# Fourteen expert tiles moved from the expert stage into the last fourteen attention groups

## The reference

```python
B, T, D, H = 8, 512, 256, 16            # batch, tokens, width, heads (16 wide each)
x  = hidden_states                                              # float16
a  = layernorm(x)
q, k, v = heads((a @ wq.T + bq) / 4), heads(a @ wk.T + bk), heads(a @ wv.T + bv)
s  = q @ k.T + causal mask (-10000 above the diagonal)
o  = softmax(s, float32).astype(float16) @ v
x  = x + layernorm(o @ wo.T + bo)
t  = layernorm(x)                                               # (4096, 256)
w, idx = top_k(t @ Ws + bs, 2); w = softmax(w)                  # 8 experts, 2 per token
y  = sum over the two experts e of  w_e * ((silu(t @ Wg[e]) * (t @ Wu[e])) @ Wd[e])   # F = 688
out = x + layernorm(y)
```

## Time and profile before

| what | value |
|---|---|
| median of 3 runs | 1003.47 us (1001.8 to 1004.06) |
| profiled execution, its own time | 1003.02 us |
| its span | 1001.3 us |
| attention groups 18 to 31 | 334.0 to 527.5 us |
| routing of the last batch, table, first rows | 527.5 to 575.6 us |
| 39 expert tiles | 575.6 to 947 us |
| combine | from 947 us |

### The profile page before, as it was taken

One profiled execution on the slowest core, in us unless ns is written; L12 is line 12 of the kernel. 1 busy time (PEld: TensorE's weight loads), 2 busy tenths in 40 slices (PEclk: granted clock), 3 DMA queues, 4 the chain that ended last, 5 costly groups with the idle time before them and its releaser, 6 DMA issues. The chain is left out here.

```text
span 1001.3 us, 22338 instructions
## 1 busy us (share of the span) xinstructions
PE 824.3 (82%) x6606; PEld 472.7 (47%) x6607; DVE 670.9 (67%) x2625; ACT 549.9 (55%) x1007; POOL 414.9 (41%) x428
## 2 busy tenths in 40 slices
PE   3488787799999999999982099999999999999800
PEld 1122232233333333333331087877877877877600
DVE  5667788888888988888864345555555555555535
ACT  4588877665565565556561044555555455455325
POOL 3565645562534534253445322333323323333316
PEclk9555555555555555555555599999999999999955
DMA  5344232228000101000011242323323323233164
GB/s 160 117 126 129 88 112 65 70 79 301 29 27 23 33 17 38 2 17 27 15 30 33 79 112 39 47 36 43 43 36 47 42 37 47 37 42 47 22 199 147
DMA packets 69219, 66.17 MB, mean 66 GB/s; under 512 B 5536, under 2 KB 62752, under 8 KB 69152
## 3 DMA queue, kind: packets, MB, share of 16 engines
q1 hardware_dynamic: 55872, 50.86, 16.7%
q0 software_dynamic: 13280, 14.49, 10.6%
HBM read 34.04 MB, written 31.29 MB: 65 GB/s over the span
## 5 line engine op out<-in xcount | busy, mean ns | idle before, releaser
L580 ACT ACTIVATE pT<-bank 128x512 f16<-128x512 f32 (+1 forms) x384 | 200.4, 530 | 161.9 <-PE bank L949 160.0
L691 DVE CUSTOM_DVE_ANT_0 unused<-bank,mask 128x384 f16<-128x384 f32 (+3 forms) x512 | 234.6, 483 | 73.9 <-PE bank L940 71.4
L1231 POOL DMA_INDIRECT expert_rows<-y_sb,dest x78 | 121.5, 1558 | 263.4 <-DVE y_sb L1350 224.1
L949 PE MATMUL bank<-qT,kT 32*128 32x384 f16 (+3 forms) x512 | 203.0, 449 | 23.8 <-ACT pT L580 23.6
L940 PE MATMUL bank<-kT,qT 32*128 32x384 f16 (+3 forms) x512 | 201.0, 446 | 16.8 <-DVE nmax L691 15.9
L1390 PE MATMUL bank<-xT,gu_part 128*128 128x256 f16 (+1 forms) x1716 | 202.7, 276 | 4.8 <-issue 3.8
L1390 PEld LDWEIGHTS bank<-xT,gu_part 128*128 (+1 forms) x1716 | 168.7, 100 | 36.8 <-issue 7.7
L1415 PE MATMUL bank<-wd_part,h 128*128 (+2 forms) x1326 | 163.6, 273 | 1.2 <-ACT h L1268 0.2
L482 POOL TENSOR_SCALAR_AFFINE_SELECT pT<-pT 128x512 f16<-128x512 f16 x128 | 79.8, 635 | 155.6 <-ACT pT L580 155.1
L1415 PEld LDWEIGHTS bank<-wd_part,h 128*128 128x128 f16 (+2 forms) x1326 | 117.2, 97 | 37.5 <-issue 24.5
L1268 ACT ACTIVATE h<-hid 128x512 f16<-128x512 f32 (+2 forms) x156 | 81.7, 523 | 89.0 <-DVE hid L1330 86.6
(11 more groups left out here) (150 smaller groups left out, 925.9 us busy)
## 6 DMA issues: line engine op xcount, KB each, us to landing
expert_rows<-clear SPq DMA_DIRECT2D x1, 8192.0 KB, 26.8
stage<-wg SPq DMA_DIRECT2D x8, 688.0 KB, 4.0
stage<-wu SPq DMA_DIRECT2D x8, 688.0 KB, 4.1
stage<-wd SPq DMA_DIRECT2D x8, 640.0 KB, 4.3
xin<-dispatch_rows SPq DMA_DIRECT2D x39, 130.0 KB
ys<-expert_rows SPq DMA_DIRECT2D x16, 256.0 KB, 6.0
out<-res SPq DMA_DIRECT2D x16, 256.0 KB, 2.1
x_sb<-x SPq DMA_DIRECT2D x8, 256.0 KB
```

The source lines that it names most:

```text
L580: sc.activation(pT[:, lo:hi], ST_BANK[i % 2][:, 0:hi - lo], ACT.Exp, scale=1.0 / INV_SCALE).then_inc(p_ready, 1)
L691: last = v.tensor_tensor_reduce(out=unused[:, i % 2, at:at + n], in0=S_BANK[i % 2][:, at:at + n], in1=mask[:, T - n:T], scale=-1.0, scalar ...
L949: last = mm(ST_BANK[i % 2][:, at:at + n], kT[32 * j:32 * j + 32, g, P * kt:P * (kt + 1)], qT[32 * j:32 * j + 32, g, P * kt:T], start=True, ...
L1231: gp.indirect_dma_start(out=ys_dram[:, :], in_=y_sb[j][:, t, :], in_offset=None, out_offset=bass.IndirectOffsetOnAxis(ap=dest[j][:, t:t + ...
```

## The change

Groups are counted through: group 18 (`FIRST_TILE`) is batch 4, g = 2. In each of the groups 18 to 31 one expert tile is computed inside the group's steps; the expert stage has the remaining 25 tiles.

- In even steps 2c PE makes gate and up products of chunk c of the tile (six chunks) into one bank, `X_BANK`; ACT writes tanh(gate / 2) to `hid`; in step 2c + 1 DVE multiplies (tanh + 1) by gate (`gate`) and, at that step's end, by up (`product`), with which Silu times up is done. The next chunk's products wait for `product`, since the bank is one.
- ACT rounds to float16 in steps 4, 8, 10 and 0 of the next group, POOL takes the rest (`tile_low`), PE makes the down product in steps 7, 9, 11 and in 1, 3, 5 of the next group. ACT scales the result, POOL adds it to the result rows in DRAM (`store_tile`), reads the destinations and shares (`take_tile`), and SP loads the rows (`load_tile`), one buffer.
- The three banks for projections become one in these groups; q, k, v, maxima, transposes and the output projection get one odd step each.
- A planner on DVE (`plan`, once a batch from batch 3 on) picks whole tiles of 256 rows from what has been routed and remembers how far each expert was used (`next`). The later table starts from there.
- In all groups the norm is one DVE pass less: (x - mean) * rstd in one instruction, the mean copied by POOL. The output projection is taken from PSUM by ACT and not by DVE.
- `ys_dram` is cleared as before, in batch 2; the first early store waits for it.

```diff
+FIRST_TILE = 4 * G + 2
+EARLY_TILES = G * B - FIRST_TILE
+LATER_TILES = TILES - EARLY_TILES
...
+        TILE_AT = ({"q": (1,), "k": (3,), "v": (5,), "max": (7,), "attT": (9,), "xnT": (11,)},
+                   {"y0": (1,), "y1": (3,), "q": (5,), "max": (7,), "k": (9,), "v": (11,)},
+                   {"q": (1,), "k": (3,), "v": (5,), "max": (7,), "xn2T": (11,)},
+                   {"logits": (1,), "q": (3,), "k": (5,), "max": (7,), "ranks": (9,), "v": (11,)})
+        AT_TILE_T = 6
+        AT_UP = {2 * c: c for c in range(FC)}
+        AT_DOWN, AT_LATE_DOWN = {7: 0, 9: 1, 11: 2}, {1: 3, 3: 4, 5: 5}
...
 SP
+                def load_tile(n):
+                    sp.wait_ge(plan_ready, PLAN_OF[n] + 1)
+                    sp.wait_ge(keep["scattered"], 16 * TOP * QT * (PLAN_OF[n] + 2))
+                    if n:
+                        sp.wait_ge(tile_xT_mm, n)
+                        sp.wait_ge(tile_taken, n)
...
 POOL
+                    gp.tensor_copy(mean[:, :], mv[:, :, 0]).then_inc(mean_ready, 1)
...
+                def tile_low(n, m):
+                    pool.wait_ge(h1_ready, 4 * n + m + 1)
+                    cols = slice(0, 2 * TS) if m < CP - 1 else slice(0, TS)
+                    gp.tensor_tensor(h2[:, m, cols], hid[:, m, cols], h1[:, m, cols], ALU.subtract
+                                     ).then_inc(h2_ready, 1)
...
                             cut(G * b + g, c)
+                            n = G * b + g - FIRST_TILE
+                            if n >= 0:
+                                tile_low(n, c)
+                            if n >= 1 and c == 0:
+                                store_tile(n - 1)
+                            if n >= -1 and n + 1 < EARLY_TILES and c == 1:
+                                take_tile(n + 1)
...
 ACT
+                def tanh(n, c):
+                    rows, cols = slice(0, P if c < FC - 1 else FR), slice(TS * (c % 2), TS * (c % 2) + TS)
+                    act.wait_ge(up_mm, FC * n + c + 1)
...
+                    sc.activation(hid[rows, c // 2, cols], X_BANK[rows, 0:TS], ACT.Tanh, scale=0.5 / WSCALE
+                                  ).then_inc(tanh_ready, 1)
...
 DVE
-                        last = v.tensor_scalar(cen[:, t, :], src[:, t, :], mv[:, t, 0:1], None, ALU.subtract)
...
-                        last = v.tensor_scalar(dst[:, t, :], cen[:, t, :], rstd[:, t:t + 1], None, ALU.mult)
+                        last = v.tensor_scalar(dst[:, t, :], src[:, t, :], mean[:, t:t + 1], rstd[:, t:t + 1],
+                                               ALU.subtract, ALU.mult)
...
+                def gate(n, c):
...
+                    dve.wait_ge(tanh_ready, FC * n + c + 1)
+                    v.scalar_tensor_tensor(hid[rows, c // 2, cols], hid[rows, c // 2, cols], 1.0, X_BANK[rows, 0:TS],
+                                           ALU.add, ALU.mult).then_inc(gate_ready, 1)
...
+                def product(n, c):
...
+                    dve.wait_ge(gate_ready, FC * n + c + 1)
+                    v.scalar_tensor_tensor(hid[rows, c // 2, cols], other, 0.5 * HSCALE / WSCALE / WSCALE,
+                                           hid[rows, c // 2, cols], ALU.mult, ALU.mult).then_inc(hid_ready, 1)
...
+                            n = grp - FIRST_TILE
+                            if n >= 1 and i == 1:
+                                tile_last_low(n - 1)
+                            if n >= 0 and i % 2:
+                                gate(n, i // 2)
...
+                            if n >= 0 and i % 2:
+                                product(n, i // 2)
...
 PE
+                def tile_up(n, c, col):
+                    if c == 0:
+                        pe.wait_ge(tile_xT_out, n + 1)
+                    if n == 0 and c == 0:
+                        pe.wait_ge(k_taken, EARLY_USES[1])
+                    else:
+                        pe.wait_ge(hid_ready, FC * n + c)
...
+                            if n >= 0 and i in AT_UP:
+                                tile_up(n, AT_UP[i], expert[0] * (KD * GU))
+                            if n >= 0 and i in AT_DOWN:
+                                tile_down(n, AT_DOWN[i], expert[0] * (FC * D))
+                            if n >= 1 and i in AT_LATE_DOWN:
+                                tile_down(n - 1, AT_LATE_DOWN[i], before_ * (FC * D))
...
 experts
-    NTILE = TILES
+    NTILE = LATER_TILES
```

More of the change, by code:

```diff
@@ L119, in build @@
             "fill": sb(outer, "fill", [P, E], F32),
[L120 removed]
+            "next": sb(outer, "next", [P, E + 1], F32),
+            "ys_early": sem("ys_early"),
         }
@@ L188, in attention @@
         std = sb(stack, "std", [P, QT], F16)
-        cen = sb(stack, "cen", [P, QT, D], F16)
+        mean = sb(stack, "mean", [P, QT], F32)
         rstd = sb(stack, "rstd", [P, QT], F32)
         stage = [sb(stack, f"stage{j}", [P, FC * D], F32) for j in range(2)]
+        hid = stage[0][:, :].rearrange("p (c n) -> p c n", c=CP)
+        h1, h2 = [stage[1][:, :].bitcast(F16)[:, part * FC * D:(part + 1) * FC * D].rearrange("p (c n) -> p c n", c=CP)
+                  for part in range(2)]
         logit = sb(stack, "logit", [P, QT, E], F32)
@@ L313, in attention, with add @@
-        USE = uses_of()
+            use, count = {}, [0, 0, 0]
+            def add(what, of, home):
+                use[what, of] = (home, count[home])
+                count[home] += 1
+            add("xnT", 0, 2)
+            for g in range(G - 1):
+                for what in ("q", "k", "v"):
+                    add(what, g, HOME[what])
+            add("max", 0, 0)
+            for grp in range(G * B):
+                for i in range(NF):
+                    for what in NAMES:
+                        if steps(grp, what)[:1] == (i,) and subject(grp, what) is not None:
+                            add(what, subject(grp, what), HOME[what] if grp < FIRST_TILE else 0)
@@ new lines, in uses_of, with wait_filled, wait_taken @@
+            early = tuple(count)
+            for what in ("attT", "y0", "y1", "xn2T", "logits", "ranks"):
+                add(what, B - 1, TAIL_HOME[what])
+            return use, early
+        USE, EARLY_USES = uses_of()
+        MISC = (Q_BANK, K_BANK, M_BANK)
+        FILLED, TAKEN = (q_filled, k_filled, m_filled), (q_taken, k_taken, m_taken)
+        def wait_filled(eng, key):
+            home, n = USE[key]
+            eng.wait_ge(FILLED[home], n + 1)
+        def wait_taken(eng, key):
+            home, n = USE[key]
+            eng.wait_ge(TAKEN[home], n + 1)
@@ L1010, in ranks, with tile_transpose @@
                                start=(s == 0), stop=(s == t))
                     for s in range(QT):
-                        last = mm(TOTAL, ones[:, :], both[:, s, :], start=(s == 0), stop=(s == QT - 1))
-                    last.then_inc(k_filled, 1)
+                        last = mm(TOTAL_OF[1 - USE[key][0]], ones[:, :], both[:, s, :], start=(s == 0), stop=(s == QT - 1))
+                    last.then_inc(filled(key), 1)
+                def tile_transpose(n):
+                    pe.wait_ge(tile_in, 16 * n + 16)
+                    pe.wait_ge(att_out, FIRST_TILE + n - 1)
+                    rows = xin[:, :, :].bitcast(F16)
+                    for k in range(KD):
+                        for t in range(TS // P):
+                            last = nc.tensor.transpose(TILE_XT16[:, TS * k + P * t:TS * k + P * (t + 1)],
+                                                       rows[:, t, P * k:P * (k + 1)], ident[:, :])
+                    last.then_inc(tile_xT_mm, 1)
@@ new lines, in tile_up @@
+                def tile_up(n, c, col):
+                    if c == 0:
+                        pe.wait_ge(tile_xT_out, n + 1)
+                    if n == 0 and c == 0:
+                        pe.wait_ge(k_taken, EARLY_USES[1])
+                    else:
+                        pe.wait_ge(hid_ready, FC * n + c)
+                    if c < FC - 1:
+                        sources = ((X_BANK[:, 0:TS], c * P, P), (X_BANK[:, TS:2 * TS], GU_UP + c * P, P))
+                    else:
+                        sources = ((X_BANK[0:UP_ROWS, 0:TS], GU_LAST, UP_ROWS),)
+                    for target, at, width_ in sources:
+                        for s in range(2 * KD):
+                            k, part = s // 2, s % 2
+                            last = mm(target, keep["gu"][part][:, bass.ds(col + (k * GU + at), width_)],
+                                      tile_xT[n % 2][:, k, :], start=(s == 0), stop=(s == 2 * KD - 1))
+                    last.then_inc(up_mm, 1)
```

694 lines of the change are left out of this document (440 added, 254 removed), and 3 rows, old and new, of the table EARLY_AT.

## The result

The changed kernel takes 1016.8 us (median of 4 runs, 1015.5 to 1021.1), the kernel before 1002.9 us beside it: a ratio of 1.0146 (95% interval 1.0113 to 1.0179). The forecast was 956 us. The time lies in the range of the prediction and on the other side of no change.

A forecast was written before the change was run, and what follows sets the result against it. PE was taken to set the pace in both stages. Twelve groups of 20.8 us and two of 16 (+88.1), fourteen tiles fewer (-133.1) and the tail (-2) gave -47 us: 956 us, range 923 to 1040.

The forecast's parts named there:

- what a tile saves: Expert stage: a tile takes 9.51 us, so fourteen fewer tiles take 133.1 us less.
- VectorE's sum: Tile groups: VectorE's work adds up to 17.8 us a group; VectorE alone gives a lower bound of 242 us for fourteen.
- no table loads in attention: Attention: Tanh and Exp share one table set, so ACT loads no table there.
- rival 4: Attention: Tanh and Exp don't share a table, 12 loads of 1.28 us a group, about 1095 us; chance 0.03.
- PE and its clock: Tile groups: PE needs 17.7 us a group at the upper clock, 31.3 at the lower; the clock was expected to rise.
- Rival 2: Tile groups: the clock alternates, half the time low, as PE waits at every second step; 1030 us, 975 to 1065; chance 0.12.
- the ring: Tile groups: with one gate and up bank, DVE stands 0.35 us a pair of steps; 3.3 us a pair, 19.9 a group.
- Rival 3: Tile groups: clock high, couplings cost 0.45 us more a pair, 23.5 us a group; 993 us, with twice that 1025; chance 0.08.
- the signs that the prediction named for being wrong: Last fourteen groups: clock at 0.50, ACT loading tables, or PE's waits being for POOL's cuts or low parts.
- the signs for the forecast: Last fourteen groups: clock 1.00, pitch about 21 us, DVE busy about 85%, PE idle before `product`; expert tiles 9.5 us.
- the tail: After the last group: two DVE passes less (1.75 us), POOL's copy adds 0.4, table instructions shorter; -2 us.
- groups 0 to 17: Attention before the tiles: PE stays the bound, DVE's relief of 1.2 us a group lies beside it; nothing, bounds 0 and -5 us.

The follow-up runs named there:

- the best kernel: Changed kernel with gate and product before maxima, tile 13's store between the roots, norms earlier, third-group adds behind the second cut, value projection taken first: 967.0 us.
- fillers: Changed kernel plus four matmuls without use, in the scores' free bank, ahead of five of the six up products of a group: 1008.8 us.
- The norms' list: Changed kernel with only the norms of the second half of the block placed one or two steps earlier (AT_FINISH): 1023.9 us; groups 0 to 17 289.9 us.
- Ten tiles: Changed kernel with ten tiles inside attention in place of fourteen, from group 22, planned from batch 4, the load's wait one batch later: 1020.4 us.

## Why the prediction was wrong

**Right: what a tile saves.** 25 expert tiles are left, (948.96 - 720.49) / 24 = 9.52 us each, 9.51 forecast; 132.3 us saved of 133.1:

```profile
720.49 0.60 ACT L1590 ACTIVATE xT<-bank 128x512 f16<-128x512 f16 x1 [21.78 <-PE bank L1710]
...
948.96 0.57 ACT L1590 ACTIVATE xT<-bank 128x512 f16<-128x512 f16 x1
```

**Right: VectorE's sum.** 242 us forecast for the fourteen groups, 239.1 measured; gate and product 0.42 each, as taken from the earlier trace rows.

**Right: no table loads in attention.** Between 0.8 and 721 us the trace has no table load. A Tanh takes 0.38 us, and rival 4 is out.

**Right in part: PE and its clock.** 17.7 us forecast at the upper clock; the best kernel has 254.2 / 14 = 18.2 at 0.96. The clock did rise with the first tile and was 0.89, not the 1.00 on which the sum was built. Rival 2 had the alternation and its reason, that PE waits a little at every second step, with half the time low; it is 22%. By the rival's own prices 22% is some 32 us over the forecast, by the rows above it is some 27; fillers that bring it to 10% of the time give back 8 us net. The Trainium skill, TensorE: Matmul & The Clock Gate, "A second HAM failure mode: psum-queue depth-cycling", describes short idling between groups of matmuls that makes the clock go down and up; the trace agrees with that, in eleven falls behind waits of 1.2 to 2.4 us, and not with the share of time that rival 2 gave it. One reading of the prediction was loose: ahead of the fall at 24 to 28 us PE ran scores mostly, but eight value projections and one of k too.

**Wrong: the ring, the step that failed.** The prediction said "DVE stands some 0.35 us in each pair of steps: 2 x 17.8 / 12 + 0.35 = 3.3 us". VectorE stood 324.0 - 239.1 = 84.9 us in the fourteen groups, 1.0 us a pair, and the pair took 3.93. The prediction let VectorE have all of the even step's work while PE multiplied and counted no order in the odd one. In the odd step the maxima stand between the scores and `gate`, and the norms, the plan or the value projection between `gate` and `product`; PE's next up products wait for all of it, and VectorE's next maxima stand behind those. And the waits that this makes on PE, 39.2 us in all, went with falls of the clock, which the sum had left at 1.00. Of the 42 us that the fourteen groups are over the forecast, some 27 are the low clock by the estimate above, and some 16 are left at the upper clock. The bare round is 3.2 us, as the timeline shows, and the other work of the odd step comes on top. 20.8 us a group became 23.6, and for the last two groups 16 became 20.4. Turning the order of two instructions gives back 28 us of the 42, and with the waits behind it mended the fourteen groups take 279.8 us, where 281.6 were forecast for the order as it stood.

What came was a mixture of rivals 2 and 3, in place of the forecast. Rival 3 (993 to 1025, couplings in each pair) has 23.5 us a group, and that it meets the measured 23.6 is luck: it held the clock high, and it named the late cuts and the late value projection, which were the smaller couplings. (With the price doubled its own sum gives 1029, not 1025.) Of the signs that the prediction named for being wrong, none came: the clock was not 0.50, no table was loaded, PE's waits were not mainly for GpSimd. What missed were the signs for the forecast, clock 1.00 (0.89), 21 us a group (23.6) and VectorE busy about 85% (74%).

**Wrong: the tail, "-2".** It is +7.3. The passes were counted and GpSimd's queue was not: tile 13's store stands ahead of eight scatters and the root. Its order is worth 6.2 us in the profile and 5 in the median.

**Wrong: groups 0 to 17, "nothing, bounds 0 and -5".** It is +6.8, with PE busy 249.8 us against 248.2, so 5 of it is idle time. The prediction looked at VectorE's sum alone and not at the new places in `AT_FINISH`. The norms' list is worth 2.2 us of it. Ten tiles, with the plan a batch later, are 2.8 us shorter there, nearly all in groups 13 and 14, where the changed kernel's first plan runs. The rest is open.

**Open.** How the loss divides exactly between the clock and the round: the split is an estimate, since no run holds the clock up without adding work to PE. In the best kernel, 24.4 us at the low clock, the same estimate leaves some 12 us to it. Open too is whether a second bank for gate and up would end the round altogether. The gate half of the bank written while `product` still reads the other half was not tried: two engines would be in one bank at the same time.

## What to carry to other kernels

Where two in-order queues hand work to each other, don't price the round by the sums of the two engines: write down one round in the order of both queues, with everything that stands between the two instructions that the other engine waits for. Put those two first in their step. Where the clock can fall, a wait of PE costs more than its length: here waits of 1.2 to 2.4 us were followed by 3 to 10 us at half the clock. And before work moves into a dense stage, list what its slow neighbours (here the adds by an indirect DMA, 1.6 us each) will stand ahead of on every queue, the tail's too.

## What the runs showed of the hardware

A few small VectorE instructions of the plan were lengthened beside GpSimd, and the prediction had them at 0.18 to 0.42 us. By form, in groups 18 to 31 and the tail of the changed kernel:

```profile
L1047 DVE TENSOR_TENSOR_SCAN cum_early<-one_early,new_tiles 128x8 f32<-128x8 f32 x3 | 2.9, 977 | 0.0
L1042 DVE TENSOR_TENSOR stock<-fill,next 128x8 f32<-128x8 f32 x3 | 2.7, 916 | 0.0
...
L1002 DVE TENSOR_TENSOR prow<-row,pick 128x32 f32<-128x32 f32 x10 | 1.3, 173 | 0.0
```

One of them, with GpSimd's queue at the same time:

```profile
429.97 2.41 DVE L1042 TENSOR_TENSOR stock<-fill,next 128x8 f32<-128x8 f32 x1
...
430.01 1.23 POOL L610 TENSOR_SCALAR_AFFINE_SELECT pT<-pT 128x512 f16<-128x512 f16 x2
431.19 1.15 POOL L626 TENSOR_TENSOR stage<-stage 128x512 f16<-128x512 f32 x1
```

An addition of 8 columns took 2.41 us, where the same line took 0.15 to 0.19 us in the other four batches, and ended with GpSimd's subtraction (L626), at 432.4. The scan (L1047) took 1.89 and 0.87 us in two batches and also ended with an L626 each time, 0.17 us in two others. `gate`, with one operand in a PSUM bank, took 0.40 to 0.42 us throughout. The Trainium skill, SBUF — State Buffer, "Who interferes with whom", has the port pair that the two engines share as an exclusive lock, and a VectorE instruction with two inputs in SBUF among those that contend with a GpSimd instruction that reads SBUF; these rows agree, and show it standing through three GpSimd instructions in a row. It is no large part of the loss: all forms of the plan add up to 15.8 us in the fourteen groups, 1.1 a group where 1.0 was forecast. In the round, though, such an instruction costs its length: the 2.41 us stood between one `product` and the next, PE's wait for that next one, until 435.26, was the longest (2.44 us), and the clock fell right then.
